# First attention: the value projection is placed ahead of the key projection in every unit that makes both

## The reference

```python
q = einsum('btm,mhd->bthd', x, w_aq); k = ...w_ak; v = ...w_av   # 8 heads of 128
q = _rope(q); k = _rope(k)
s = einsum('bihd,bjhd->bhij', q, k) / D_HEAD
s = s - INF_APPROX * (i < j)                                     # causal
p = softmax(s); o = einsum('bhij,bjhd->bihd', p, v)
r = einsum('bihd,hdm->bim', o, w_ao)                             # added to x
```

## Time and profile before

| | before |
|---|---|
| times of three executions | 4946.10, 4948.01, 4949.84 us |
| span of the profiled execution | 4944.1 us (3.9 us under the median; the page gives no other time of it) |
| PE busy over the span | 3835.4 us (78%) |
| DVE / ACT / POOL busy | 3465.1 (70%) / 2341.8 (47%) / 2386.9 (48%) us |
| mean granted TensorE clock | 0.900 of full speed |
| first attention | 16.7 us (first input transposes) to 498.4 us (end of its last addition to the stream) |

### The profile page before, as it was taken

How to read it: one execution, slowest core, us unless ns; L and a number is a source line. 1 busy time by engine, 2 the same in 40 slices (tenths; PEclk the granted TensorE clock), 3 DMA queues, 4 the chain that set the end, 5 groups by cost and what they waited for, 6 DMA issues and landing times. The chain is left out here.

```text
span 4944.1 us, 90876 instructions
## 1 busy us (share of the span) xinstructions
PE 3835.4 (78%) x25840; PEld 2735.3 (55%) x25840; DVE 3465.1 (70%) x9524; ACT 2341.8 (47%) x5537; POOL 2386.9 (48%) x3900
## 2 busy tenths in 40 slices
PE   7889797779999799568869937567775887799365
PEld 5666565656666466456646626422332665466265
DVE  7887775666666676566658856669998664588566
ACT  3444464355666466234436624345553454366243
POOL 5666442534344442446643354367776662233453
PEclk9999898789999899679979959779998999899698
DMA  6000332100000232133323311212121330133113
GB/s 234 0 0 1 112 124 76 52 20 1 0 0 1 72 124 94 39 124 107 107 80 117 110 38 47 73 48 65 63 62 64 114 117 28 51 120 112 36 46 87
DMA packets 244547, 341.24 MB, mean 69 GB/s; under 512 B 26976, under 2 KB 187120, under 8 KB 243120
## 3 DMA queue, kind: packets, MB, share of 16 engines
q1 hardware_dynamic: 230960, 309.19, 18.8%
q0 software_dynamic: 13184, 27.22, 1.6%
HBM read 182.77 MB, written 147.26 MB: 67 GB/s over the span
## 5 line engine op out<-in xcount | busy, mean ns | idle before, releaser
L522 DVE TENSOR_REDUCE l0att_rowmax<-l0att_S 128x2 f32<-128x512 f32 x512 | 339.8, 687 | 125.2 <-PE l0att_S L701 122.9
L893 POOL TENSOR_TENSOR wb_prob<-wb_prob,wb_rden 128x128 f32<-128x128 f32 (+1 forms) x512 | 248.2, 506 | 360.7 <-DVE wb_rden L1070 360.3
L522 DVE TENSOR_REDUCE l1ffn_rowmax<-l1ffn_S 128x2 f32<-128x512 f32 x512 | 337.6, 686 | 87.2 <-PE l1ffn_S L701 83.1
L1983 POOL TENSOR_TENSOR ssm_hc<-core_AW_all,ssm_Cs 128x512 f32<-128x512 f32 x256 | 320.8, 1268 | 131.2 <-DVE core_AW_all L2129 98.1
L1434 POOL DMA_INDIRECT results<-e_y,e_back x220 | 213.7, 971 | 289.4 <-DVE e_y L1662 269.9
L935 ACT ACTIVATE wb_prob<-wb_biased,wb_nmax 128x128 f32<-128x128 f32 (+1 forms) x512 | 228.6, 447 | 236.0 <-DVE wb_nmax L1063 233.6
L2228 PE MATMUL ssm_Y<-ssm_hc,core_ident 128*128 128x512 f32 x512 | 287.8, 672 | 56.8 <-POOL ssm_hc L1983 31.1
L2129 DVE TENSOR_TENSOR_SCAN core_AW_all<-core_AW_all,ssm_U 128x512 f32<-128x512 f32 x256 | 310.6, 1213 | 1.0 <-ACT core_AW_all L2072 0.6
L701 PE MATMUL l1ffn_S<-l1ffn_K,l1ffn_Q 128*128 128x512 f32 x512 | 251.0, 494 | 75.1 <-DVE l1ffn_rowmax L522 42.3
L1775 PE MATMUL e_H<-e_xT,e_W1s 128*128 128x128 f32 x1760 | 252.0, 288 | 70.2 <-issue 50.6
L701 PE MATMUL l0att_S<-l0att_K,l0att_Q 128*128 128x512 f32 x512 | 248.6, 489 | 60.4 <-DMA l0att_K<-bounce 47.5
(11 more groups left out here) (498 smaller groups left out, 11511.3 us busy)
## 6 DMA issues: line engine op xcount, KB each, us to landing
bounce<-l0att_parts SPq DMA_DIRECT2D x128, 256.0 KB, 2.8
bounce<-l1ffn_parts SPq DMA_DIRECT2D x128, 256.0 KB, 2.8
ssm_Cs<-c_rows SPq DMA_DIRECT2D x128, 256.0 KB, 3.1
routed<-core_Y SPq DMA_DIRECT2D x8, 2048.0 KB, 24.8
l0att_Q<-bounce SPq DMA_DIRECT2D x128, 128.0 KB
l0att_K<-bounce SPq DMA_DIRECT2D x128, 128.0 KB
bounce<-l1att_parts SPq DMA_DIRECT2D x64, 256.0 KB, 2.8
l1ffn_Q<-bounce SPq DMA_DIRECT2D x128, 128.0 KB
```

The source lines that it names most:

```text
L522: dve.tensor_reduce(out=rowmax[:, jp, qt, 2 * pair:2 * pair + 2], in_=S[a % 2][:].rearrange("p (j k) -> p j k", j=2)[:, :, 0:keys(qt)], op ...
L893: ins = pool.tensor_tensor(out=prob[:, w_ % NP, a:b], in0=prob[:, w_ % NP, a:b], in1=rden[:, w_ % NP, n:n + 1].to_broadcast([P, b - a]), o ...
L1983: pool.tensor_tensor(out=hc[:, u % 4], in0=hs[:, u % 4], in1=Cs[:, n % 4], op=ALU.mult)\
```

## The change

The two projections of an odd unit change places, for the first attention alone:

```diff
-    pieces = [("q",), ("k", "v")] if HS == 1 else [("q",), (), ("k",), ("v",)]
+    pieces = [("q",), ("v", "k")] if HS == 1 else [("q",), (), ("k",), ("v",)]
```

## The result

The changed kernel takes 4960.84 us (median of 7; 4957.96 to 4971.98), the kernel before, run beside it, 4946.10 (median of 7; 4938.09 to 4949.84). The ratio is 1.0034, 95% interval 1.0024 to 1.0045: 12 to 22 us slower; the medians differ by 14.7. Forecast were 4967 us, by 19.3 us more than before.

What follows compares the result with a forecast made beforehand. PE was taken as nearly gapless, with a 6.04 us key loop over ACT just covered; the values make it 6.93. Turns sum 14.2 + 1.4 + 3.7 = 19.3 us more, so 4967 us, range 4952 to 4978.

Steps and rivals of the forecast that it cites:

- The loop and its size: Regular step: key rotation 2.10, to weighing 2.12, values 0.76, keys 0.89, rotation 1.06; 6.93 us instead of 6.06 to 6.12; 80%.
- No wait of the keys for the queries' bank: Regular step: query rotation ends 4.95 us behind the key rotation's start, keys start at 5.87, so they do not wait.
- Unit 5 gives back 0.52: Unit 3 to 5, statistics on DVE: 8.29 us falls to 7.77 as DVE's idle time before the query rotation goes.
- Unit 7 unchanged: Unit 5 to 7, with the normalization: 8.55 us before, all on DVE behind a late maximum; no change.
- Unit 9 loses 0.35: Unit 7 to 9: output transposes gain 0.28, keys come 0.89 later; rotation at 304.77 instead of 304.42, loss 0.35 us.
- Unit 11 to 13 gains 0.83: Input transposes start 0.65 instead of 2.22 us behind the key rotation's start; next key rotation at +7.32 instead of 8.15.
- The sum: First attention longer by 14.2 us in six turns, 1.4 in the first and 3.7 in the last: 19.3 us.
- The start: Start of the block: the first turn starts with no weighing, DVE sets the pace as before; no loss counted there.
- a PE without gaps and one loop over ACT that is just covered: Kernel before: PE nearly gapless with 6.1 us of work a step; the key loop over ACT takes 6.04 us, just covered.
- The clock: Rival: idling lowers PE's clock in regular steps, 68 us more, 5035 us; 4%. The forecast itself kept 1.00 there.
- no DMA moves in this stretch: First attention: no DMA moves there that could hide the longer block, so the blocks behind start when it ends.

Runs made afterwards that it cites:

- e7: The change with only two of the four value multiplies in units 1 to 11 (half of those heads' values not computed); 4948.64 us, one run.
- e3: The change, with ACT copying the transposed probabilities of unit w-3 ahead of the exponentials of unit w; 4929.44 us, ratio 0.9973 to before.
- e10: The change with ACT's copy ahead of the exponentials and half of the value multiplies in units 1 to 11; 4926.14 us, one run.
- e6: Against the change: values issued in the even unit behind the queries, ACT's copy ahead of the exponentials, values emptied in the odd unit; 4920.60 us, 0.9964 to before.
- e8: The kernel before with half of the value multiplies in units 1 to 11 (half of those heads' values not computed); 4937.12 us, one run.
- e9: The kernel before with ACT's copy ahead of the exponentials and half of the value multiplies in units 1 to 11; 4946.67 us, one run.
- e4: The kernel before, with ACT's copy of the transposed probabilities ahead of the exponentials; ratio 0.9984 to before.
- e5: Against the change: values issued in the even unit behind the queries, and ACT's copy ahead of the exponentials; 4904.82 us, 0.9931 to before.

## Why the prediction was right

- **The loop and its size.** The mechanism was the one forecast, and so was its size. Forecast 6.93 us as 2.10 + 2.12 + 0.76 + 0.89 + 1.06; measured 6.93. e7 shows the term of the values in it, e3 the part over ACT.
- **No wait of the keys for the queries' bank.** Right: no such wait in the trace of the change; it appears where the loop over ACT is cut (e10).
- **Unit 5 gives back 0.52.** Measured 8.29 to 7.69: 0.60. Unit 7 unchanged: 8.55 to 8.52.
- **Unit 9 loses 0.35.** 9.81 to 10.27, 0.46. The output transposes start 2.03 us behind the start of the key rotation and not 1.94: 0.19 us were gained, not 0.28.
- **Unit 11 to 13 gains 0.83.** 8.15 to 7.16, 0.99. The transposes came at +0.60 (forecast +0.65), the query rotation at +3.77 (+3.81), the keys' at +7.16 (+7.32).
- **The sum.** Forecast 14.2 for six turns, 1.4 for the first, 3.7 for the last. Measured, with the turns parted as in the forecast (behind the key rotation of unit 15), 13.3, 1.0 and 3.7, and 1.6 at the start of the block, up to unit 1. That the sum, 19.6, is so near to 19.3 is in part luck: the 1.6 make up for the 1.3 that the turns fell short. Single long places nearly cancel in the six turns: 0.65 and 1.21 us in before, less 0.33 at a short one, and 1.18 in the change.
- **The start, which I had counted as nothing, was a term missed.** The values stand ahead of the keys there too: the first key rotation comes 3.31 us behind the first query rotation and not 2.13 (24.09 and 27.40 in the change, 22.82 and 24.95 before). In e3, e6 and e7, with the values ahead of or apart from the keys and the first query rotation at 22.4 to 23.0 us, unit 1 comes 0.9 to 1.1 us later than before; in e8 and e9, with the order of before and the first query rotation at 22.6 and 23.0 us, it comes within 0.1 us of before. So about 1 us of the 1.6 is the change's. The rest goes, most likely, with the first query rotation at 24.09 (in e4, with the order of before and this rotation at 24.34 us, unit 1 comes 0.8 us later than before): it waits for a projection that nothing in the change touches, and that took 2.07 us here against 1.12 in e3 (timelines of PE in the change and in e3):

```profile
21.97 2.07 PE L1155 MATMUL wa_F<-wa_hT,core_AW_all 128*128 128x512 f32 x2 [0.69 <-ACT wa_wvo L987]
...
21.84 1.12 PE L1155 MATMUL wa_F<-wa_hT,core_AW_all 128*128 128x512 f32 x2 [0.69 <-ACT wa_wvo L987]
```

  The place of this rotation differs from 22.4 to 24.3 us over the traces. About 19 of the 19.6 us are the change's.
- **What was not whole: the view of what had set the step.** The prediction names a PE without gaps and one loop over ACT that is just covered. e8 shows that PE's work did not hold the step alone, and e9 that without the loop over ACT, and with less work on PE, it still stays at 6.05 us: the two-bank loop, which the prediction does not have, is enough for that. Whether the other loops, summed at 6.03 to 6.05 us, would have held it without this one is not shown. It did not touch the number, since the new loop is longer than all of them.
- **The clock.** By the row, the granted clock was 1.00 in the regular steps of the change with 0.8 us of idling in each, and 0.97 over the block (before 0.96). The swing between both clocks for which the prediction cites the Trainium skill does not show there.
- **A reading that was wrong without harm:** "no DMA moves in this stretch". DMA moves up to about 100 us (share 0.55 from 60 to 100 us before) and not behind it; no wait of the loop is for a DMA.

## What to carry to other kernels

When several engines work on a shared software pipeline, add up every loop through the semaphores, also those that are covered: here an edit that adds no work put 0.89 us into a loop that was 0.01 us short of the step, and all but those 0.01 us were lost. The order of two independent pieces on one engine matters by who waits for each; put first the one that the busiest engine waits for, and put the other where that engine has other things to do. Where one idle time vanishes and a larger one appears at another place of the same engine, the loop has changed, not the work.

## What the runs showed of the hardware

Less work on TensorE made single places longer. In e9, with half of the value multiplies, unit 13 takes 9.82 us in every second turn and 8.15 in the others; in e4, the same kernel with whole values, it takes 8.15 in all. The timeline of PE in e9 at a long place and at a short one, and then the windows of the same kernel (busy time of PE, PEld, DVE, ACT and POOL, then the granted clock):

```profile
309.95 0.61 PE L1152 MATMUL wa_F<-wa_wvo,wa_hT 128*128 128x128 f32 x4
312.64 0.63 PE L1142 MATMUL wa_F<-core_ident,wa_yn 128*128 128x128 f32 x4 [2.08 <-DVE wa_rt L1039]
313.10 1.01 PE L1168 MATMUL wa_S<-wa_kT,wa_qT 128*128 128x128 f32 x4
...
253.92 0.63 PE L1142 MATMUL wa_F<-core_ident,wa_yn 128*128 128x128 f32 x4 [2.08 <-DVE wa_rt L1039]
254.39 0.82 PE L1168 MATMUL wa_S<-wa_kT,wa_qT 128*128 128x128 f32 x4
```

```profile
310.00:318.00 8.00, 5.92 (x27) 4.47 (x26) 3.70 (x14) 3.42 (x11) 4.34 (x6) 0.79 0.00 0
312.60:315.60 3.00, 2.96 (x14) 2.59 (x15) 0.72 (x5) 1.41 (x5) 1.70 (x3) 0.67 0.00 0
253.90:256.90 3.00, 2.98 (x18) 2.37 (x19) 0.72 (x5) 1.87 (x5) 1.89 (x3) 1.00 0.00 0
```

The values take 0.61 us where they took 1.05, and PE idles 2.08 us in front of the transposes, where the kernel before has 1.41 and e4 1.64 at the same place. At the long place the granted clock is 0.67 over the 3 us from the transposes on, partly the level of 1.2 GHz; at the short place, behind the same 2.08 us, it is 1.00. The same shows in e5 at unit 9, which takes 8.33 us in most turns and 6.69 in one (timeline of PE in e5, a long place and the short one):

```profile
225.95 1.13 PE L1155 MATMUL wa_F<-wa_hT,core_AW_all 128*128 128x512 f32 x2 [2.04 <-DVE wa_rt L1039]
226.91 1.68 PE L1152 MATMUL wa_F<-wa_wvo,wa_hT 128*128 128x128 f32 x8
228.38 1.49 PE L1168 MATMUL wa_S<-wa_kT,wa_qT 128*128 128x128 f32 x4
...
172.60 1.12 PE L1155 MATMUL wa_F<-wa_hT,core_AW_all 128*128 128x512 f32 x2 [2.03 <-DVE wa_rt L1039]
```

The windows of e5 around both:

```profile
223.00:226.00 3.00, 0.96 (x8) 0.72 (x6) 2.75 (x9) 1.36 (x5) 0.99 (x3) 1.00 0.00 0
226.00:229.00 3.00, 3.00 (x13) 2.52 (x14) 2.97 (x9) 0.99 (x4) 2.22 (x3) 0.69 0.00 0
172.60:175.60 3.00, 3.00 (x18) 2.42 (x19) 2.97 (x9) 0.99 (x4) 2.24 (x3) 1.00 0.00 0
```

Here 2.04 us of idling are followed by a granted clock of 0.69 over 3 us, and the scores take 1.49 us; 2.03 us in another turn are followed by 1.00. In the kernel before, PE idles 1.80 to 1.82 us in unit 6 of the six middle turns. In five of them the clock is 1.00 over the 3 us there; in one it was 0.71 over 3 us, and unit 7 took 9.19 us instead of 8.55. After 3.89 us it was 0.51 in one turn. The timeline of PE in the kernel before at both kinds of unit 6, and a window of it:

```profile
287.52 0.70 PE L1188 MATMUL wa_O<-wa_probT,wa_V 128*128 128x256 f32 x2 [1.82 <-ACT wa_probT L962]
...
227.72 0.70 PE L1188 MATMUL wa_O<-wa_probT,wa_V 128*128 128x256 f32 x2 [1.82 <-ACT wa_probT L962]
```

```profile
227.50:230.50 3.00, 2.78 (x9) 1.79 (x10) 1.84 (x8) 2.02 (x7) 2.13 (x4) 0.71 0.00 0
```

So the same idle time in front of one place is followed by either clock, and the unit is 1.6 to 1.7 us longer (0.6 in before) where the clock is the low one: the extra time goes with the clock and not with that wait. What makes it fall in one turn and not in the next was not tried.
